# Padding the edges sorted by destination to 256 per tile, with two chunks summed in one PSUM bank

## The reference, cut to what matters

```python
src, trg = (edge_index[0], edge_index[1])
proj = (x @ Wp.T).reshape(-1, H, FO)                    # H = 8 heads of FO = 32
s = scores_src[src] + scores_trg[trg]
s = jax.nn.leaky_relu(s, negative_slope=0.2)
s = s - jnp.max(s)
exp_s = jnp.exp(s)
denom = jax.ops.segment_sum(exp_s, trg, num_segments=N)
weighted = proj[src] * attn[:, :, None]                 # attn = exp_s / denom[trg]
out = jax.ops.segment_sum(weighted, trg, num_segments=N)
```

## Time and profile before

| | before |
|---|---|
| median of 3 runs | 7969.41 us (7962.21 to 7973.39) |
| the profiled execution, first to last instruction | 7942.4 us |
| stage `attend`: first gather issued, last rows landed and taken up, last addition done | 1247.1, 3382.3, 3395.1 us |
| its 1612 gathers: POOL busy | 1633.9 us |
| its 1612 additions: DVE busy | 687.4 us |

### The profile page before, as it was taken

How to read it: one execution, slowest core, us unless ns; L and a number is a source line. 1 busy time by engine, 2 the same in 40 slices (tenths; PEclk the granted TensorE clock), 3 DMA queues, 4 the chain that set the end, 5 groups by cost and what they waited for, 6 DMA issues and landing times. The chain is left out here.

```text
span 7942.4 us, 87092 instructions
## 1 busy us (share of the span) xinstructions
PE 5581.7 (70%) x25066; PEld 3810.3 (48%) x25066; DVE 5151.1 (65%) x11656; ACT 1874.7 (24%) x4564; POOL 3471.0 (44%) x3440
## 2 busy tenths in 40 slices
PE   5877773555555655528799788887999999960991
PEld 2446652333333433314454334443777777750661
DVE  6467777888888877764367566666666666660332
ACT  0333332222223332212134200000222222220220
POOL 0000005777777777700000455555666667625006
PEclk8998886677777777759899899998998999965995
DMA  4100004444555555510013322222333333332223
GB/s 145 42 26 1 1 1 105 124 123 124 125 127 130 134 130 129 126 38 0 17 78 132 112 68 70 71 72 72 89 95 87 89 95 95 92 77 80 63 64 107
DMA packets 310174, 665.89 MB, mean 84 GB/s; under 512 B 77964, under 2 KB 173950, under 8 KB 302701
## 3 DMA queue, kind: packets, MB, share of 16 engines
q0 software_dynamic: 180352, 455.22, 22.7%
q1 hardware_dynamic: 129367, 205.30, 7.5%
HBM read 546.51 MB, written 113.55 MB: 83 GB/s over the span
## 5 line engine op out<-in xcount | busy, mean ns | idle before, releaser
L2026 POOL DMA_INDIRECT ag_rows<-table,row_src x1612 | 1594.9, 989 | 2007.2 <-POOLq L2813 1052.5
L1123 POOL DMA_INDIRECT at_rows<-table,row_dst x1612 | 1633.9, 1014 | 491.0 <-issue 448.9
L1289 PE MATMUL at_p_a<-at_rows,at_hot 128*125 128x264 f32 x3224 | 1137.0, 511 | 997.3 <-issue 976.8
L1289 PEld LDWEIGHTS at_p_a<-at_rows,at_hot 128*125 128x125 f32 x3224 | 708.6, 246 | 1184.9 <-issue 1045.2
L1252 DVE TENSOR_TENSOR acc<-acc,at_p_a 125x264 f32 x1612 | 687.4, 426 | 244.3 <-PE at_p_a L1289 101.4
L2388 PE MATMUL mo_p_e<-ag_rows,ag_hot 128*125 128x256 f32 x2192 | 651.0, 422 | 265.0 <-DVE acc L2232 231.5
L2232 DVE TENSOR_TENSOR acc<-acc,mo_p_e 125x256 f32 x1096 | 459.3, 419 | 498.7 <-PE mo_p_e L2388 308.0
L2388 PEld LDWEIGHTS mo_p_e<-ag_rows,ag_hot 128*125 128x125 f32 x2192 | 392.0, 199 | 480.3 <-DVE acc L2232 376.3
L2136 DVE TENSOR_TENSOR mo_prod<-mo_far,mo_twice 125x256 f32<-125x256 f32 x1600 | 580.1, 419 | 50.9 <-issue 44.3
L1075 POOL PARTITION_ALL_REDUCE sb_top<-sb_top x1 | 0.4, 397 | 1220.5 <-DVE sb_top L1046 1220.5
L1239 DVE TENSOR_TENSOR at_rows<-at_rows 128x1024 f32<-128x1024 f32 x496 | 496.9, 1022 | 21.8 <-ACT at_rows L1171 21.5
(11 more groups left out here) (475 smaller groups left out, 9944.2 us busy)
## 6 DMA issues: line engine op xcount, KB each, us to landing
at_wide<-node_t SPq DMA_DIRECT2D x124, 406.2 KB
table<-rt_row SPq DMA_DIRECT2D x50, 1000.0 KB
at_rows<-table,row_dst POOLq DMA_INDIRECT x1612
ag_rows<-table,row_src POOLq DMA_INDIRECT x1612, 2.8
moe_in<-ones SPq DMA_DIRECT2D x1, 13440.0 KB
ex_space<-moe_in SPq DMA_DIRECT2D x105, 128.0 KB, 2.2
moe_out<-ex_space SPq DMA_DIRECT2D x105, 128.0 KB, 1.7
table<-row SPq DMA_DIRECT2D x50, 128.9 KB
```

The costliest lines, as they stand in the source:

```text
L1123: pool.indirect_dma_start(out=rows[n % 3][:, g, :], out_offset=None, in_=m.table0, in_offset=bass.IndirectOffsetOnAxis(ap=row_i[:, n * G + ...
L1289: pe.matmul(p_a[k % BANKS][0:P, 0:TW], hot[n % 2][:, g, :], rows[n % 3][:, g, :], start=True, stop=True).then_inc(s_agg, 1)
L2026: pool.indirect_dma_start(out=rows[:, i % RING, j, :], out_offset=None, in_=m.table1, in_offset=bass.IndirectOffsetOnAxis(ap=row_i[:, 2 * ...
```

## The change

The padding unit for the sort by destination becomes 256, so that two chunks in a row, a pair, belong to one tile. `attend` works on groups of `GD` = 12 chunks, that is `PD` = 6 pairs; there are `ND` = 139 groups, `CD` = 1668 chunks. The two chunks of a pair are summed by PE in one bank (`start` on the first, `stop` on the second), so that DVE adds 834 times, one tile number is loaded for a pair, and ACT copies 6 rows of scores in a group. A group has three parts of four chunks; the third is scaled after the first addition, and the one-hot matrices are made after the additions of pairs 1, 3 and 5. With the inputs' destinations 804 pairs (1608 chunks) are in use; the last 60 chunks hold row 6250 alone, and so does the second chunk of 18 pairs before them. The sort by source keeps chunks of 128 and groups of 13.

```diff
+GD = 12
+PD = GD // 2
+ND = -(-((E + NT * (2 * LANES - 1)) // (2 * LANES)) // PD)
+CD = ND * GD
...
+                        unit = (LANES, 2 * LANES)[s]
...
-                        dve.tensor_scalar(need[:, :], need[:, :], -1.0, float(LANES), ALU.mult, ALU.add)
+                        dve.tensor_scalar(need[:, :], need[:, :], -1.0, float(unit), ALU.mult, ALU.add)
...
-                        dve.tensor_scalar(bits(upper[0:1, 0:FS // 2]), bits(k[0:1, 0:FS // 2]), shift + 7, 63,
-                                          ALU.logical_shift_right, ALU.bitwise_and)
+                        dve.tensor_scalar(bits(upper[0:1, 0:CD // 2]),
+                                          bits(k[0:1, 0:CD]).rearrange("o (c two) -> o c two", two=2)[:, :, 0],
+                                          shift + 7, 63, ALU.logical_shift_right, ALU.bitwise_and)
...
-                for n in range(NG):
+                for n in range(ND):
                     for q, gs in parts:
                         if n >= 3:
-                            pool.wait_ge(s_agg, (n - 3) * G + gs[-1] + 1)
+                            pool.wait_ge(s_agg, (n - 3) * PD + gs[-1] // 2 + 1)
...
-                    for g in range(G):
+                    for g in range(PD):
                         act.copy(near[u][:, g, :], m.terms[:, bass.ds(tiles[g], 1), :].rearrange("p o w -> p (o w)")
                                  ).then_inc(s_near, 1)
...
-                    for g in range(G):
-                        if not (isinstance(n, int) and n == 0 and g == 0):
-                            dve.wait_ge(s_acc, n * G + g)
-                        dve.wait_ge(s_agg, n * G + g + 1)
+                    for g in range(PD):
+                        k = n * PD + g
+                        if k > 0:
+                            dve.wait_ge(s_acc, k)
+                        dve.wait_ge(s_agg, k + 1)
                         row = acc[:, bass.ds(tiles[g], 1), :].rearrange("p o w -> p (o w)")
-                        dve.tensor_tensor(row, row, p_a[(n * G + g) % BANKS][0:P, 0:TW], ALU.add).then_inc(s_acc, 1)
-                        if g in (1, 3):
-                            scale_rows(2 + g // 2)
-                        for q, gs in parts:
-                            if g == gs[-1] and n + 2 < NG:
-                                one_hot(n + 2, n % 2, gs)
+                        dve.tensor_tensor(row, row, p_a[k % BANKS][0:P, 0:TW], ALU.add).then_inc(s_acc, 1)
+                        if g == 0:
+                            scale_rows(2)
+                        if g % 2 == 1 and n + 2 < ND:
+                            one_hot(n + 2, n % 2, parts[g // 2][1])
...
-                        if k >= BANKS:
+                        if g % 2 == 0 and k >= BANKS:
                             pe.wait_ge(s_acc, k - BANKS + 1)
-                        pe.matmul(p_a[k % BANKS][0:P, 0:TW], hot[n % 2][:, g, :], rows[n % 3][:, g, :],
-                                  start=True, stop=True).then_inc(s_agg, 1)
-                        if g in after and n + 2 < NG:
+                        mm = pe.matmul(p_a[k % BANKS][0:P, 0:TW], hot[n % 2][:, g, :], rows[n % 3][:, g, :],
+                                       start=g % 2 == 0, stop=g % 2 == 1)
+                        if g % 2 == 1:
+                            mm.then_inc(s_agg, 1)
+                        if g in after and n + 2 < ND:
                             fetch(n + 2, after[g])
```

More of the change, by code:

```diff
@@ L1020, in rounds, with tiles_of @@
     return (n // 2 + 1) * each if isinstance(n, int) else (n - u) * (each // 2) + each
[L1023 to L1025 removed]
+def tiles_of(nc, engine, tile_of, n, k):
+    return nc.values_load_multi_w_load_instructions(tile_of[0:1, bass.ds(n * k, k)], engines=[engine],
                                                     min_val=0, max_val=NT - 1,
@@ L1091, in attend @@
         sb, ps, sem = m.scope(nc, ctx)
-        rows = [sb(f"at_rows{u}", [128, G, TW], F32) for u in range(3)]
-        hot = [sb(f"at_hot{u}", [128, G, P], F32) for u in range(2)]
-        wide = [sb(f"at_wide{u}", [P, G * 128], BF16) for u in range(2)]
+        rows = [sb(f"at_rows{u}", [128, GD, TW], F32) for u in range(3)]
+        hot = [sb(f"at_hot{u}", [128, GD, P], F32) for u in range(2)]
+        wide = [sb(f"at_wide{u}", [P, GD * 128], BF16) for u in range(2)]
         minus_p = sb("at_minus_p", [P, 1], F32)
-        hot_t = sb("at_hot_t", [P, G, 128], BF16)
-        zs = sb("at_zs", [128, G, H], F32)
-        own = sb("at_own", [128, G, H], F32)
-        diff = sb("at_diff", [128, G, H], F32)
-        near = [sb(f"at_near{u}", [P, G, 4 * H], BF16) for u in range(2)]
+        hot_t = sb("at_hot_t", [P, GD, 128], BF16)
+        zs = sb("at_zs", [128, GD, H], F32)
+        own = sb("at_own", [128, GD, H], F32)
+        diff = sb("at_diff", [128, GD, H], F32)
+        near = [sb(f"at_near{u}", [P, PD, 4 * H], BF16) for u in range(2)]
         p_f = [ps(f"at_p_f{k}", [128, 512]) for k in range(2)]
@@ L1107, in attend @@
             "s_near", "s_hot", "s_hot_t", "s_fetch", "s_diff", "s_exp", "s_msg", "s_agg", "s_acc"))
-        parts = [(q, list(range(4 * q, min(4 * q + 4, G)))) for q in range((G + 3) // 4)]
+        parts = [(q, list(range(4 * q, min(4 * q + 4, GD)))) for q in range((GD + 3) // 4)]
         NQ = len(parts)
@@ L1273, in fetch @@
                         mm = pe.matmul(p_f[u][:, 4 * H * g:4 * H * g + 4 * H], hot_t[:, g, :],
-                                       near[u][:, g, :], start=True, stop=True)
-                    if gs[-1] == G - 1:
+                                       near[u][:, g // 2, :], start=True, stop=True)
+                    if gs[-1] == GD - 1:
                         mm.then_inc(s_fetch, 1)
-                fetch(0, range(G))
-                fetch(1, range(G))
-                after = {g: range(2 * (g - 5), min(2 * (g - 5) + 2, G)) for g in range(5, 12)}
-                for n in range(NG):
-                    for g in range(G):
-                        k = n * G + g
+                fetch(0, range(GD))
+                fetch(1, range(GD))
+                after = {g: range(2 * (g - 5), min(2 * (g - 5) + 2, GD)) for g in range(5, 11)}
+                for n in range(ND):
+                    for g in range(GD):
+                        k = n * PD + g // 2
                         if g % 4 == 0:
@@ L2226, in edge_work @@
                             if g == 0:
-                                tiles = ahead if n > 0 else tiles_of(nc, mybir.EngineType.DVE, m.tile_src, 0)
+                                tiles = ahead if n > 0 else tiles_of(nc, mybir.EngineType.DVE, m.tile_src, 0, G)
                             if 2 * i + j > 0:
@@ L2233, in edge_work @@
                             if g == G - 2 and n + 1 < NG:
-                                ahead = tiles_of(nc, mybir.EngineType.DVE, m.tile_src, n + 1)
+                                ahead = tiles_of(nc, mybir.EngineType.DVE, m.tile_src, n + 1, G)
                         if i % 2 == 0 and 2 * i + HOTS < CH:
```

58 lines of the change are left out of this document (24 added, 34 removed).

## The result

| | before | after |
|---|---|---|
| median (lowest to highest) of 4 runs each | 7971.4 us (7962.21 to 7975.79) | 8103.39 us (8087.9 to 8115.91) |
| ratio to before, 95% interval | | 1.0167 (1.0153 to 1.0182) |
| profiled execution, span | 7942.4 us | 8114.2 us |
| stage `attend`, first gather to end of last addition | 2148.0 us | 2298.8 us |

The change makes the kernel 1.7% slower, 132 us in the medians. The direction was forecast; the time lies above the forecast (8048) and above the range (7996 to 8095).

The account below looks back on a forecast made before the run. POOL's full gather queue was taken as the bound, the DMA engines for the final padding. Gathers +18.2, padding +63.3, tail -2 and unpacking -1 gave +78.5 us on a 7969.4 us median: 8048 us, range 7996 to 8095.

Parts of the forecast that it names:

- POOL sets the pace, and saved additions are worth nothing: In `attend`, POOL's gather queue is full at 1.25 us a gather plus delays by DVE (holds); 778 fewer additions gain nothing.
- The first rival: In `attend`, DVE was the bound, so its shorter chain frees the gathers to bare 1.25 us: 7943 us; chance 0.05.
- Padding at the end, +63.3: At the end of the stage, 60 padding gathers instead of 22, DMA-bound at 1.667 us each: +63.3 us.
- The rival that padding costs no more than other rows: In the final padding only the count matters: 49 us instead of 63, kernel at 8033 us; chance 0.12.
- The 18 chunks of padding inside the order: Among the ordinary gathers, they cost the queue 0.4 us each at most, which POOL hides; if not, +8 us.
- The tail: After the last landing, DVE's remaining 12.8 us shrink with 6 additions and one chunk less: -2 us.
- the start: In unpacking, four one-partition instructions become two and three wide ones grow by 3.5%: -1 us.
- the wait for pairs: In each group DVE's first addition waits for two chunks, not one: a few tenths of a us, inside DVE's slack.
- Ordinary gathers, +18.2: Before the final padding, 1608 gathers instead of 1590, half at 1.342 us and half at 1.288: +18.2 us.
- 1.29 to 1.34 us a gather: Sign of a right prediction: POOL's rate per gather after the change; under 1.27 would be wrong.
- The bounds of that step: For ordinary gathers: -32 us at 15.4 us a group, up to +75 at 16.4 beside the exchange and 16.0 elsewhere.
- holds grow: Rival: the exchange falls where a group's last gathers are issued, delaying them more: +135 us, 8104 us; chance 0.15.

Follow-up runs that it names:

- after_single: The changed kernel with the addition for each chunk back (1668 additions), its order and padding kept: 8084.32 us, ratio 1.0145 to the kernel before.
- after_spread: The changed kernel with the last 60 chunks, all padding, fetching mostly different rows instead of one row: 8074.31 us, ratio 1.0139 to the kernel before.
- before_again: An unchanged copy of the kernel before, profiled and run beside it: 7963.0 us, ratio 1.0004.

## Why the prediction was right and wrong

**POOL sets the pace, and saved additions are worth nothing:** right. The gaps stayed at 0.30 us, and after_single, with 355 us more on DVE, was no slower. The first rival, that DVE was the bound, is out, and with it what ranking engines by their busy share would have said.

**Padding at the end, +63.3:** right, +67.0 measured; after_spread shows its cause, which the prediction had taken from the share of the DMA engines. The rival that padding costs no more than other rows is out. POOL itself was not slowed by it: it issued the padding at its own pace, and the DMA engines finished late. Of the +67.0, 50.0 us are the time to issue 38 more gathers (77.5 for 27.5 us), and 17.0 come of the landings, which end 28.5 us after the last issue and not 11.5. The 18 chunks of padding inside the order cost no more than others: no gap ahead of a gather in use is over 0.31 us.

**The tail, the start, the wait for pairs:** -2.1 for -2; +2.0 for -1, which says nothing, since the first gather comes anywhere from 1243.0 to 1249.1 us in the profiles from the usual chips; no new wait of POOL for PE appeared before the padding.

**Ordinary gathers, +18.2:** wrong, +85.8. The failed step is the sentence "I take the measured rates of the first and the last stretch, the nearest rows there are". In the first stretch of the kernel before, 1.342 us a gather were read as the price of work beside the exchange. But in that price the exchange's own holds are almost nothing (6.9 us in all), because of its phase; the rest are holds by scalings, 36 us of which went when the exchange did. With the new order these terms moved apart: the exchange +56.2 us, the one-hot matrices +37.0, the scalings -34.0, and the rates came out at 1.410 and 1.303 for 1.342 and 1.288, which over 804 gathers each is the 67 us missing. So the sign "1.29 to 1.34 us a gather" failed in the first stretch. That the exchange held next to nothing showed in the trace: the exchange of 2010.19 lies beside gathers of 0.95 and 1.02 us. The prediction listed which gathers were long, but not which two-input instructions held none, and why. It treated holds as a rate that carries over, where they depend on phase, which a change of the order sets anew. Without knowledge of the phase the exchange is better priced by the mean over phases, 0.57 us, with 0 and 1.1 as bounds; it measured 0.94 a group. By the same reasoning a one-hot instruction (window 0.67 - 0.12 = 0.55 us) costs 0.55 x 0.55 / 2 / 1.25 = 0.12 us on average, three a group 0.36, and the trace after has 0.33 a group beside the exchange and 0.22 elsewhere; before they held nothing, since no gather began inside one but at its very end. The mean is no forecast, however: two scalings in a row and a third would cost 0.57 + 1.10 x 1.10 / 2 / 1.25 = 1.05 us a group by it, and they held 0.49. With all three terms the mean puts the gathers in use at some +141 us, for +85.8 measured and +18.2 forecast. What fixes the phases of the scalings, and of 40 of the 58 exchanges, stays open.

One reading was off besides: the held gathers of the earlier trace rows end 0.81 and 0.83 us after their scaling, not about 0.95, so a hold ends 0.12 us before the instruction does. No term of the sum used it.

**The bounds of that step:** too narrow as well. The upper bound was 16.4 us a group, from one group seen. Measured were 16.92. The bound of 16.0 for the other groups held (15.65). The rival "holds grow", which named the exchange falling on the last gathers, gave 8104 us and had a chance of 0.15. It is the case that came, but 8103.4 for 8104 is luck: the stage grew by 151 us, not 135, and the medians' difference was 132. What counted was where in a gather's 1.25 us the exchange begins, not beside which gathers of the group.

**From the profile to the median:** the 27 us between the profiled execution and the median, which were taken "as unchanged", aren't a fixed part. The span after was 1.7 us under its own time (8114.2, 8115.91), and the profile of before was simply of a short execution; the same code behind the stage took 4547 us there and 4565 in before_again. It costs nothing in the sum, since a difference of stages was added to a median, but it explains why the spans differ by 172 us and the medians by 132.

## What to carry to other kernels

When an engine's queue is full, price each edit by what it does to that queue, in number and in length of its entries: 56 more gathers cost 90 us here, and 778 fewer additions on another engine gained none. A stall that depends on where two periodic streams meet has no rate that carries over: reckon it by the mean over phases, bound it by zero and the whole window, and best remove what makes it (here an operand moved to PSUM, worth 119 us of the changed stage). The mean is a guard against taking a lucky phase for a price; for the scalings here it was over twice what came. Padding should not point all lanes at one row: that was worth 24 us.

## What the runs showed of the hardware that was not expected

- A gather under way is not held, and doesn't hold DVE: the exchange's first instruction began 0.25 us into a gather and took its usual 1.21 us. In the changed kernel's trace 462 scalings and exchange instructions of 1.22 us began inside a gather, and none took over 1.23 us. A gather that begins inside such an instruction ends 0.82 us after that instruction's end, as if it began anew 0.12 us before that end. The Trainium skill, "SBUF — State Buffer", section SBUF: two separate sides, has the pair of ports go for the whole instruction to whichever starts first, with the other fully blocked (for a DVE instruction with two SBUF inputs, against a POOL instruction that reads SBUF). These traces bear that out in one direction alone, and show nothing of a DVE instruction blocked by a gather.
- A two-input instruction of DVE with one input in PSUM holds no gather, at the same length (1.22 us): holds of 103.4 us became 0.4.
- Many lanes fetching one row: 60 gathers in 106.0 us at 95.1% of the DMA engines, and in 80.2 us at 40.2% with different rows; POOL issued them in 77.5 and 77.4 us.
- The load of a group's tile numbers on DVE took 2.93 us for 13 numbers and 1.39 us for 6, 0.23 us for each. The Trainium skill, "Runtime: NRT & Kernel Launch", section Instruction fetch mechanics, gives about 0.2 us for each register that such a load (TENSOR_LOAD) fills, and describes it for loads from HBM; here the numbers lie in SBUF, and the trace agrees nearly.
- In the runs where the kernel before took 8425 us or more, PE's signals came late, in the case shown over 4 us after the ends of its matmuls as the trace models them. What the gaps ahead of gathers have over 0.30 us came to 162 to 366 us there, and to at most 38 us in the other runs.
